# Three passes over the edges of a graph network: vector-engine instructions of eight chunks issued as four of two

## The reference, cut to what matters

```python
# layer 0, twice
edge_feat = concatenate([h[src], h[dst]])
messages  = relu(edge_feat @ msg_W1 + msg_b1) @ msg_W2 + msg_b2
att       = sigmoid(relu(edge_feat @ att_W1 + att_b1) @ att_W2 + att_b2)
aggregated = segment_sum(messages * att, dst)
# layer 2
attn     = einsum('ehd,ehd->eh', Q[dst], K[src]) * rel_scale[rel] / sqrt(DH)
attn_exp = exp(attn - max(attn))
out      = segment_sum(attn_exp * V[src], dst) / segment_sum(attn_exp, dst)
# layer 3, the scores
scores = einsum('ehd,ehd->eh', q[src], k[tgt]) / sqrt(16)
scores = (scores + edges @ We + be) * cons[tgt] + relu(distances @ Wd1 + bd1) @ Wd2 + bd2
```

## Time and profile before

| | |
|---|---|
| median of three timed runs | 8057.35 us |
| the profiled execution, its own time | 8061.98 us |
| its span, first to last instruction | 8060.2 us |
| PE busy | 5681.0 us, 70% |
| DVE busy | 4911.6 us, 61% |
| POOL busy | 5196.1 us, 64% |
| ACT busy | 1400.6 us, 17% |
| granted TensorE clock, mean | 0.743 of 2.4 GHz |
| DMA, mean over the span | 98 GB/s |

### The profile page before, as it was taken

The page is one execution under the profiler, slowest core; times in us unless marked ns, Lnnn a source line. Parts: engine busy times, 40 slices in busy tenths (PEclk is TensorE's granted clock), DMA queues, the critical chain, the costliest instruction groups (busy, mean ns, idle before and its releaser), DMA issues. The chain is left out here.

```text
span 8060.2 us, 144412 instructions
## 1 busy us (share of the span) xinstructions
PE 5681.0 (70%) x31732; PEld 4609.5 (57%) x31872; DVE 4911.6 (61%) x16813; ACT 1400.6 (17%) x3612; POOL 5196.1 (64%) x4817
## 2 busy tenths in 40 slices
PE   2677776588888788887789898668787874555533
PEld 1666665366766577666455554457787763333322
DVE  7788886377776577776555555346666653444454
ACT  0333333022222111111122222100000010000000
POOL 0666666277777377776388888537777733777751
PEclk6555555799999899998899999866766675555556
DMA  1444444444444244444255554324444423333320
GB/s 63 111 112 111 111 111 122 132 129 128 129 128 126 77 129 128 129 129 106 41 83 79 81 80 78 68 68 118 120 120 120 120 47 72 84 85 85 84 57 26
DMA packets 929159, 791.00 MB, mean 98 GB/s; under 512 B 580951, under 2 KB 748307, under 8 KB 927667
## 3 DMA queue, kind: packets, MB, share of 16 engines
q0 software_dynamic: 264032, 434.24, 22.8%
q1 hardware_dynamic: 649788, 342.32, 16.9%
q10 hardware_dynamic: 15264, 13.50, 0.7%
HBM read 700.00 MB, written 88.28 MB: 98 GB/s over the span
## 5 line engine op out<-in xcount | busy, mean ns | idle before, releaser
L1005 POOL DMA_INDIRECT there<-table_wide,idx x1664 | 1624.8, 976 | 780.2 <-issue 553.8
L1906 POOL DMA_INDIRECT there<-table_wide,idx x832 | 918.7, 1104 | 449.2 <-issue 253.2
L1586 POOL DMA_INDIRECT partial_sums<-row_sums1a,idx1a x632 | 1015.6, 1607 | 229.8 <-issue 202.5
L2342 POOL DMA_INDIRECT there<-table_narrow,idx x832 | 802.7, 965 | 478.4 <-issue 235.9
L1094 PE MATMUL ps<-here,hot_t 128*128 x3328 | 1003.2, 427 | 77.1 <-DVE there L1045 60.3
L649 POOL DMA_INDIRECT rec<-out_recd,posd x806 | 804.5, 998 | 389.6 <-issue 215.2
L1102 PE MATMUL ps<-relu,hot_s 128*128 128x128 f32 x3328 | 779.9, 323 | 310.7 <-DVE hot_s L1034 308.8
L1102 PEld LDWEIGHTS ps<-relu,hot_s 128*128 128x128 f32 x3328 | 579.8, 205 | 496.9 <-issue 465.5
L2422 PE MATMUL ps<-here,hot_t 128*128 x1664 | 506.8, 464 | 502.4 <-DVE prod L2367 444.6
L1519 PE MATMUL ps<-src_hot1a,edge_parts1a 128*128 128x512 bf16 (+1 forms) x4661 | 847.4, 332 | 7.5 <-DVE src_hot1a L1393 0.2
L1045 DVE TENSOR_TENSOR there<-there,ps 128x512 f32<-128x512 f32 x832 | 569.2, 684 | 354.0 <-PE ps L1094 353.4
(11 more groups left out here) (413 smaller groups left out, 10470.7 us busy)
## 6 DMA issues: line engine op xcount, KB each, us to landing
locrows<-loc_row SPq DMA_DIRECT2D x416, 256.0 KB, 3.4
krowd<-key_row SPq DMA_DIRECT2D x201, 256.0 KB
src_rows1a<-src_row SPq DMA_DIRECT2D x79, 512.0 KB
there<-table_wide,idx POOLq DMA_INDIRECT x2496, 3.2
lrowd<-lo_row SPq DMA_DIRECT2D x201, 128.0 KB
attr_raw<-in_edge_attr SPq DMA_DIRECT2D x201, 128.0 KB
there<-table_narrow,idx POOLq DMA_INDIRECT x832, 2.5
rec<-out_recd,posd POOLq DMA_INDIRECT x806
```

Of the source, the lines that this page charges most:

```text
L1005: nc.gpsimd.indirect_dma_start(there[:, j, q, :], None, table, bass.IndirectOffsetOnAxis(idx[:, j, q:q + 1], 0)).then_inc(gathered[j][q], 16)
L1586: nc.gpsimd.indirect_dma_start(sums[q % TABLES], bass.IndirectOffsetOnAxis(idx[:, j, q:q + 1], 0), out[:, j, q, :], None, compute_op=ALU.a ...
L1906: nc.gpsimd.indirect_dma_start(there[:, j, q, :], None, table, bass.IndirectOffsetOnAxis(idx[:, j, q:q + 1], 0)).then_inc(gathered[j][q], 16)
L2342: nc.gpsimd.indirect_dma_start(there[:, j, q, :], None, table, bass.IndirectOffsetOnAxis(idx[:, j, q:q + 1], 0)).then_inc(gathered[j][q], 16)
```

## The change

Every instruction of VectorE that made a 128 x 1024 tile in these places becomes four of 128 x 256 (two chunks each). In `values` each of the four raises `placed`, so `placed` now counts four for each group; POOL's wait is scaled to it, and PE waits four times for each group, before chunks 0, 2, 4 and 6, instead of once. `PIECE` is 2 and `PIECES` is 4. The semaphore `hots` is raised by the last piece alone, as before once for each group.

```diff
@@ layer 0, hot_nodes
-                nc.vector.tensor_scalar(hot_t[:, j % 2, :], rows[:, j % 2, :], k["part"][:, 0:1], None, ALU.is_equal).then_inc(hots, 1)
+                for at in range(0, U * P, 2 * P):
+                    last = nc.vector.tensor_scalar(hot_t[:, j % 2, at:at + 2 * P], rows[:, j % 2, at:at + 2 * P], k["part"][:, 0:1], None, ALU.is_equal)
+                last.then_inc(hots, 1)
@@ layer 2, GpSimd and the start of VectorE
-                    pool.wait_ge(placed, i * RING + (j + 1))
+                    pool.wait_ge(placed, i * (RING * PIECES) + ((j + 1) * PIECES))
...
-            dve.sem_inc(placed, RING)
+            dve.sem_inc(placed, RING * PIECES)
@@ layer 2, targets
-                nc.vector.tensor_scalar(hot_t[:, j % 2, :], rows[:, j % 2, :], k["part"][:, 0:1], None, ALU.is_equal).then_inc(hots, 1)
+                for at in range(0, U * P, PIECE * P):
+                    last = nc.vector.tensor_scalar(hot_t[:, j % 2, at:at + PIECE * P], rows[:, j % 2, at:at + PIECE * P], k["part"][:, 0:1], None, ALU.is_equal)
+                last.then_inc(hots, 1)
@@ layer 2, places
-                nc.vector.tensor_tensor(hot_s[:, j % 2, :, :], k["iota"][:, None, :].to_broadcast([P, U, P]),
-                                        g["loc"][:, ds(i * CH + j * U, U)].rearrange("p (c o) -> p c o", o=1).to_broadcast([P, U, P]), ALU.is_equal)
+                for q in range(0, U, PIECE):
+                    nc.vector.tensor_tensor(hot_s[:, j % 2, q:q + PIECE, :], k["iota"][:, None, :].to_broadcast([P, PIECE, P]),
+                                            g["loc"][:, ds(i * CH + (j * U + q), PIECE)].rearrange("p (c o) -> p c o", o=1).to_broadcast([P, PIECE, P]), ALU.is_equal)
@@ layer 2, values
-                nc.vector.tensor_tensor(msg[:, b, :, :].rearrange("p q (h d) -> p (q h) d", h=H),
-                                        there[:, j, :, F:2 * F].rearrange("p q (h d) -> p q h d", h=H),
-                                        ex[:, b, :, :].rearrange("p q (h o) -> p q h o", o=1).to_broadcast([P, U, H, DH]), ALU.mult).then_inc(placed, 1)
+                for q in range(0, U, PIECE):
+                    nc.vector.tensor_tensor(msg[:, b, q:q + PIECE, :].rearrange("p q (h d) -> p (q h) d", h=H),
+                                            there[:, j, q:q + PIECE, F:2 * F].rearrange("p q (h d) -> p q h d", h=H),
+                                            ex[:, b, q:q + PIECE, :].rearrange("p q (h o) -> p q h o", o=1).to_broadcast([P, PIECE, H, DH]), ALU.mult).then_inc(placed, 1)
@@ layer 2, TensorE's add
-                    pe.wait_ge(placed, i * RING + (j + RING + 1))
                 for q in chunks:
+                    if q % PIECE == 0:
+                        pe.wait_ge(placed, i * (RING * PIECES) + ((j + RING) * PIECES + q // PIECE + 1))
```

More of the change, by code:

```diff
@@ L1834 @@
 FAR = 1e30
+PIECE = 2
+PIECES = U // PIECE
 def hgt_pass(nc, k, g, table, query, rec, low, ps):
```

## The result

The changed kernel took 7920.17 us (median of four runs, 7918.28 to 7922.68), the kernel before on the same chip 8056.68 (8053.37 to 8061.86): a ratio of 0.983, 95% interval 0.9813 to 0.9847.

A forecast was written before the change was run, and what follows sets the result against it. POOL's back-to-back gathers were taken to bound each pass. Gains of 75 us (layer 2) and 8 (layer 0), less 4 (layer 3), make 79, from 8061.98 to 7983, stated as 7980; the 8-in-10 range was 7930 to 8040.

The forecast's parts named there:

- The bound, the place and the mechanism: All passes: POOL's gathers set the time; in layer 2 DVE's port lock lengthens them, 1.24 us a group, chiefly under `values`.
- What the split costs DVE: DVE work added: 0.97 us a group in layer 2, 0.53 in layers 0 and 3, hidden by DVE's waits.
- the loop of DVE and PE: Rival, chance 0.12: in layer 2 this loop takes over, leaving 8020 us, or up to 8045.
- The fixed cost for each instruction: Rival, chance 0.02: DVE sets the period, so the pieces add 266 us, 8328 in all.
- What a gather still loses: Layer 2's gathers lose 0.54 us a group instead of 1.26; layer 0's 0.15 instead of 0.19, layer 3's 0.15 instead of 0.11.
- My own rule: A gather started under a DVE instruction is longer by that instruction's end less the gather's start less 0.13 us.
- the rival of the phases: Rival listed with the experiments: changed phases alone shorten the passes, whatever the pieces; no size or chance given.
- Admission between pieces: POOL slips in at the end of each DVE piece, so a gather waits only for the rest of one.
- The rival that the port isn't handed over: Rival, chance 0.05: POOL enters only when DVE's queue has a gap, so met gathers wait for all four pieces; 8195 us.
- The mark that I had set for this: Sign of a wrong forecast: gathers of 1.9 us under four pieces.
- the middle of the phases: Gain taken between 181 us (no gather meets a piece) and about +8 net (every request meets a fresh one).
- the second hold: Under the target one-hots, DVE begun within 0.46 us of a gather's start lengthens it by its end less 0.82.

The follow-up runs named there:

- e12: Kernel before with layer 0's one-hots whole with accumulator output and layer 2's `values` alone in four pieces, one signal: 7972.46 us beside 8060.45.
- e10: Changed kernel with one `placed` signal a group, in a set with late landings: ratio 1.0092 (1.0059 to 1.0125) to 9849.51 us before.
- e7: Changed kernel with pieces of one chunk (`PIECE = 1`, eight of 128x128): 7993.96 us beside 8077.48, ratio 0.9887 (0.9816 to 0.9959).
- e16: Changed kernel with `places` left whole, all else the same: 7929.80 us (one run).
- e13: Changed kernel with one `placed` signal and wait a group, layer 0's one-hots whole, layer 3's whole with accumulator output: 7958.66 us beside 8058.61.
- e14: Changed kernel with layer 1's one-hots (`match`) also in four pieces of two chunks: 7915.81 us, ratio 0.9813 (0.9791 to 0.9834).

## Why the prediction was right and wrong

**The bound, the place and the mechanism: right.** POOL issues back to back before and after, `values` was the worst meeting, and the two `tensor_tensor` count (0.795 us on 101 gathers; the last of my 102 is under `places`). The sentence of the Trainium skill (SBUF — State Buffer, Who interferes with whom) that I weighed against the change, its inference that `tensor_tensor` doesn't stall descriptor generation, is refuted by these rows and by e12, whose pieces of `values` alone gave 65 us.

**What the split costs DVE: right.** Pieces took 0.416 (`places`), 0.419 (`values`) and 0.374 us (`targets`), and four of them last 1.42, 1.43 and 1.14 us in a row: I had 1.44, 1.44 and 1.28. DVE's wait for `locrows` fell from 343.8 to 150.5 us, forecast 180, and covered it. PE's wait for `product` fell from 214.0 to 119.8 and never came onto the path, so the loop of DVE and PE did not take over. The fixed cost for each instruction decides nothing in this condition; it fits the numbers of the other one (e10), and layer 0 with pieces of one (e7).

**What a gather still loses: wrong, and this is the step that failed.** I let every request that meets a piece wait for the rest of it, 0.17 us a time (0.15 for the one-hots). My own rule says less: the wait is the rest less 0.13. I had that 0.13 in the worst case (0.42 - 0.13 = 0.29) and left it out of the mean. Besides, there is a wait only where DVE began 0.03 us ahead, 0.09 for the one-hots, which I didn't know. With a piece of 0.42 issued every 0.34 us, only starts 0.03 to 0.29 us into it cost anything, and the mean over all phases is 0.26 x 0.26 / 2 / 0.34 = 0.10; for one-hots of 0.38 every 0.30 it is 0.16 x 0.16 / 2 / 0.30 = 0.04. Both constants together are a small part of 1.2 us, and over a third of a `tensor_tensor`'s piece and over half of a one-hot's.

- Layer 2: 2 x 1.15 x 0.10 + 0.04 = 0.27 us a group, 28 us, not 56. The trace has 39 (42.5 less the gather in the ramp), 19 of them from the held ones, which this sum doesn't have.
- Layer 0: 0.04 x 208 = 8 us left under L1020, not the 31 that I had. By the count gather by gather L1019 had 33.5 us (I had 39) and L1020 has 1.8; the product next to it (L1026, now L1028) went from 15.7 to 5.5 besides, and `hot_s` (L1034, now L1036) from 2.2 to 4.4. All gathers together have 40.2 us less, against my 8, and their mean moved by 0.024 us, where I had said 0.01 at most. The product's code is untouched, so its 10 us come of another phase: that much of the rival of the phases, in the experiments, holds.
- Layer 3: I had 11 us for L2357 and 16 for its pieces; the count gives 7.4 and 0.7, and the pass's 4.5 lie within its spread.

The three together are 55 us of the miss, which is 58; layer 1's 14 and the sort's 8 the other way lie in code that I had put at zero.

**Admission between pieces: right as a rule, with a hole.** The rival that the port isn't handed over is true for 16 gathers of `places`, 19.4 us, and false for the one-hots. Under `values` no gather was held either, not even in pieces of one (e7). The mark that I had set for this, "gathers of 1.9 under four pieces", is there, with 2.1. These 16 began 0.08 to 0.12 us into the first piece. Why this start, why in pieces of one many others too, and why `places` alone, stays open.

**The phase.** I took the middle of the phases because I couldn't place them. They are not evenly spread: of the meetings with L1020 in layer 0, 131 of 157 fall where they cost 0.001 us, of those with `values` in layer 2 only 39 of 136. So that layer 0 kept 1.8 us and not 8 is luck of the phase, as far as these runs tell. A DVE instruction that waits for POOL starts right behind it, and then the two keep step; this reading fits the counts, and no run tests it alone.

## What to carry to other kernels

Where GpSimd issues gathers back to back, list the gathers that are longer than the shortest one and see which VectorE instruction began just before them: two inputs in SBUF or the fast `tensor_scalar` make them wait to its end, `tensor_reduce`, an input in PSUM or a `tensor_scalar` with an accumulator output don't. Cut such an instruction until what a piece can still cost is small (here pieces of 0.4 us, of which the first 0.03 to 0.09 us and the last 0.13 cost nothing), no further, and only while VectorE has slack; for a `tensor_scalar` an accumulator output does the same without cutting. When averaging such a rule over phases, keep its constants: they are what is left when the pieces are small.

## What the runs showed of the hardware that I had not expected

- The hold has a narrow entry. A one-hot of `tensor_scalar` begun over about 0.09 us ahead of the gather costs its end less 0.13 us; one begun later costs nothing (0.007 and 0.001 us over 45 and 131 gathers), but for the second hold that the prediction describes (27 gathers in layer 0, 5.7 us). For a `tensor_tensor` the entry is at about 0.03 us (11 gathers in e16). The Trainium skill's section named above says that whoever issues first has the pair for the whole instruction; the trace agrees but for these tenths.
- Between instructions in a row POOL is mostly let in, but 16 gathers waited out all four pieces of `places` (1.2 us), 12 in e13 and 11 in e14, and in e7 59 waited to the end of its eight.
- `tensor_scalar` with an accumulator output lasts 1.28 us for 128x1024 instead of 0.78 and lengthened none of 144 gathers.
- The same kernel took 8057 us in some sets of runs and 9733 to 9850 in others, with landings that came late and, but for a few, the same packets. There the change with one signal costs 0.7 to 0.9%; the changed kernel as it stands was not run there.
